# Convolutions of a graph network: the matmuls of a gathered group stand singly between the dense products

## The reference, cut to what matters

```
h   = x @ W                                   # 12500 nodes, 96 features
msg = dinv[row] * w * dinv[col] * h[row]      # 400,000 edges, sorted by destination
xc  = segment_sum(msg, col) + b
g   = sigmoid(x @ Wr + br)
x   = relu((1 - g) * x + g * xc)
```

## Time and profile before

| | |
|---|---|
| median of 3 runs | 11252.27 us (11244.29 to 11253.65) |
| the profiled execution | 11244.56 us, its span 11242.6 us |
| convolution stage, with both layers | about 5764 us to 11160 us of the span |
| TensorE busy over the span | 8235.0 us, 73% |
| GpSimd busy over the span | 6709.2 us, 60% |

### The profile page before, as it was taken

The page is one execution under the profiler, slowest core; times in us unless marked ns, Lnnn a source line. Parts: engine busy times, 40 slices in busy tenths (PEclk is TensorE's granted clock), DMA queues, the critical chain, the costliest instruction groups (busy, mean ns, idle before and its releaser), DMA issues.

```text
span 11242.6 us, 161615 instructions
## 1 busy us (share of the span) xinstructions
PE 8235.0 (73%) x40104; PEld 5614.5 (50%) x40104; DVE 5197.6 (46%) x17514; ACT 2896.6 (26%) x6502; POOL 6709.2 (60%) x6696
## 2 busy tenths in 40 slices
PE   5567666666767676667748888888875888888886
PEld 4334444444444444444435556555553555555554
DVE  5566666666666676666612222222231222222223
ACT  4345555555555555555300000000000000000000
POOL 4666565565566565656456666666645666666663
PEclk7678888888888888888768888888876988888887
DMA  4346566565566665656346666666664666666666
GB/s 151 81 132 175 166 175 172 167 174 168 171 174 175 172 176 172 172 168 174 128 144 230 229 236 237 228 232 233 228 205 152 232 225 235 231 233 232 232 229 204
DMA packets 1329034, 2149.88 MB, mean 191 GB/s; under 512 B 306427, under 2 KB 1079948, under 8 KB 1328700
## 3 DMA queue, kind: packets, MB, share of 16 engines
q10 hardware_dynamic: 142400, 986.64, 24.3%
q1 hardware_dynamic: 925996, 684.95, 20.7%
q0 software_dynamic: 260560, 477.49, 15.9%
HBM read 1587.45 MB, written 560.99 MB: 191 GB/s over the span
## 4 chain that ended last, share of the span: by engine, by line
PE 56%; issue 15%; another core or an unknown queue 15%; ACT 7%; DVE 3%; DMA 2%; POOL 1%; DVEq 1%; ACTq 1%; SPq 0%; POOLq 0%
PE bd L1159 30%; PE bd L1055 11%; PE sg L1146 6%; ACT blocks L1286 3%; PE pb L1044 3%; PE sg L1074 2%; PE pa L1044 2%; ACT hid L1265 2%; ACT msg L1278 1%; ACT gate_t L1271 1%; PE bd L1108 1%; PE bd L1171 0%; PE bd L1167 0%; DMA out_nodes<-s_c 0%
## 5 line engine op out<-in xcount | busy, mean ns | idle before, releaser
L909 POOL DMA_INDIRECT hid<-src_table,src_ids x3127 | 3188.8, 1020 | 2068.0 <-ACT msg L1278 1080.4
L1159 PE MATMUL bd<-ring,table_sb 128*96 128x280 f32 x13720 | 3580.3, 420 | 254.6 <-issue 145.1
L1159 PEld LDWEIGHTS bd<-ring,table_sb 128*96 128x96 f32 x13720 | 2332.5, 172 | 1408.7 <-issue 545.7
L1055 PE MATMUL bd<-one_hot_dst,one_hot_src 128*128 128x343 bf16 x8400 | 1751.2, 353 | 1449.9 <-ACT blocks L1286 1135.8
L953 POOL DMA_INDIRECT hid<-conv_table,hid x1724 | 1660.3, 963 | 1058.5 <-issue 512.4
L1055 PEld LDWEIGHTS bd<-one_hot_dst,one_hot_src 128*128 128x128 bf16 x8400 | 841.3, 108 | 2251.8 <-issue 1787.4
L1286 ACT ACTIVATE blocks<-bd 128x686 f32<-128x686 f32 x1400 | 1116.8, 798 | 2255.3 <-remote 1489.7
L953 POOL DMA_INDIRECT feat_in<-conv_table,hid x1152 | 1121.3, 973 | 618.3 <-issue 334.0
L1871 DVE TENSOR_TENSOR acc<-acc,sg 96x64 f32 x434 | 94.6, 218 | 2527.3 <-remote 1188.3
L1391 ACT ACTIVATE side_out<-bd,side_flag 96x280 f32<-96x280 f32 x70 | 34.3, 490 | 4022.5 <-issue 2294.1
L1885 DVE TENSOR_TENSOR acc<-acc,side_out 96x7 f32 x2800 | 469.6, 168 | 1256.2 <-issue 933.5
(11 more groups left out here) (226 smaller groups left out, 6957.8 us busy)
## 6 DMA issues: line engine op xcount, KB each, us to landing
ring<-adjacency ACTq DMA_DIRECT2D x980, 980.0 KB
adjacency<-blocks SPq DMA_DIRECT2D x700, 686.0 KB
attr<-in_attr SPq DMA_DIRECT2D x392, 128.0 KB
hid<-src_table,src_ids POOLq DMA_INDIRECT x3127
hid<-conv_table,hid POOLq DMA_INDIRECT x1724
feat_in<-conv_table,hid POOLq DMA_INDIRECT x1152
conv_table<-table_sb SPq DMA_DIRECT2D x28, 336.0 KB, 4.7
feat_half<-feat_keep SPq DMA_DIRECT2D x56, 168.0 KB
```

The source lines that it names most:

```text
L909: pool.indirect_dma_start(out=hid[s][:, t, :], out_offset=None, in_=src_rows, in_offset=bass.IndirectOffsetOnAxis(ap=src_ids[s // 2][:, j: ...
L1055: op = nc.tensor.matmul(bd[:, 512 * h:512 * h + HALF_Z], y[:, 1 + k, :], z[:, Z_PAD * h:Z_PAD * h + HALF_Z], start=(k == 0), stop=(k == 2))
L1159: op = nc.tensor.matmul(side_ps, table_sb[:, D * k:D * (k + 1)], ring[slot][:, :, QUAD_FANS * b:QUAD_FANS * (b + 1)], start=(k == 0), stop ...
```

## The change

Before, the eight matmuls of a group stand in a row behind a piece of seven dense products (behind pieces 1, 3, 6, 8, 10 and 13). In the changed kernel the loop runs over single products; behind every second one stands one matmul of a group. A group is thus spread over 16 products, six groups over 96, and products 96 and 97 have nothing behind them. The waits of a group stand before its first matmul, and `seg` is set by its eighth. The numbers of instructions, shapes, operands and buffers are the same, and so are the programs of the other engines.

```diff
-                    for t in range(GROUP):
-                        op = nc.tensor.matmul(sg[j][0:D, WINDOW * slot:WINDOW * (slot + 1)], conv_g[j][slot][:, t, :],
-                                              conv_s[j][slot][:, t, :], start=(t == 0), stop=(t == GROUP - 1))
-                    op.then_inc(s["seg"], 1)
+                    op = nc.tensor.matmul(sg[j][0:D, WINDOW * slot:WINDOW * (slot + 1)], conv_g[j][slot][:, t, :],
+                                          conv_s[j][slot][:, t, :], start=(t == 0), stop=(t == GROUP - 1))
+                    if t == GROUP - 1:
+                        op.then_inc(s["seg"], 1)
...
-                    for i in range(PIECES):
-                        piece(i, loaded)
-                        if i in SEGMENT_AFTER:
-                            m = SEGMENT_AFTER.index(i)
-                            unit_segment(m, u, n0)
-                            if mix and m == 0:
-                                mix_gate(h0 + u)
-                            if mix and m == 2:
-                                mix_own(h0 + u)
+                    for k in range(BLOCKS):
+                        product(k, loaded)
+                        m, turn = divmod(k, GROUP_BLOCKS)
+                        if m < UNIT_GROUPS and turn % BLOCKS_PER_TILE == BLOCKS_PER_TILE - 1:
+                            unit_tile(m, turn // BLOCKS_PER_TILE, u, n0)
+                        if mix and k == GROUP_BLOCKS:
+                            mix_gate(h0 + u)
+                        if mix and k == 3 * GROUP_BLOCKS:
+                            mix_own(h0 + u)
```

More of the change, by code:

```diff
@@ L99 @@
 RING = 7
-SEGMENT_AFTER = (1, 3, 6, 8, 10, 13)
+BLOCKS_PER_TILE = 2
+GROUP_BLOCKS = GROUP * BLOCKS_PER_TILE
 ADD_PARTS = 4
@@ L1150, in unit_segment, with segment_tile @@
-                def unit_segment(i, u, n0):
+                def segment_tile(t, k, j, m, slot, n0, s=cv[l]):
+                    if t == 0:
+                        if slot == 0 and not (isinstance(k, int) and k < 2):
+                            pe.wait_ge(s["acc"], n0 + group_of(k - 1, ACC_CREDIT))
+                        pe.wait_ge(s_rows[j][slot], rows_gathered(m, j, slot))
+                        pe.wait_ge(s["weighted"], n0 + group_of(k, slot + 1))
+                    op = nc.tensor.matmul(sg[j][0:D, WINDOW * slot:WINDOW * (slot + 1)], conv_g[j][slot][:, t, :],
+                                          conv_s[j][slot][:, t, :], start=(t == 0), stop=(t == GROUP - 1))
+                    if t == GROUP - 1:
+                        op.then_inc(s["seg"], 1)
@@ L1151, in unit_segment, with unit_tile, product @@
+                def unit_tile(i, t, u, n0):
                     k, slot = LEAD_STEPS + i // STEP_GROUPS, i % STEP_GROUPS
-                    segment(u * 2 + k, k % 2, u + k // 2, slot, n0)
-                def piece(i, loaded, s=cv[l]):
+                    segment_tile(t, u * 2 + k, k % 2, u + k // 2, slot, n0)
+                def product(k, loaded, s=cv[l]):
+                    i, b = divmod(k, PIECE_BLOCKS)
                     slot = i % RING
[L1156 to L1162, removed]
+                    if b == 0:
+                        pe.wait_ge(s_ring[slot], loaded * 32 + (16 * (i // RING) + 16))
+                    op = nc.tensor.matmul(side_ps, table_sb[:, D * k:D * (k + 1)],
+                                          ring[slot][:, :, QUAD_FANS * b:QUAD_FANS * (b + 1)],
+                                          start=(k == 0), stop=(k == BLOCKS - 1))
+                    if b == PIECE_BLOCKS - 1:
+                        op.then_inc(s["eaten"], 1)
@@ L1192, in _ @@
                         for slot in slots_of(k):
-                            segment(k, k % 2, k // 2, slot, n0)
+                            for t in range(GROUP):
+                                segment_tile(t, k, k % 2, k // 2, slot, n0)
                     with pe.Fori(0, HALVES) as u:
```

## The result

The changed kernel took 11339.97 us in the median of 4 runs (11337.22 to 11346.77), the kernel before 11248.63 in the median of 4 runs (11244.29 to 11253.65). It is slower: the medians differ by 91 us, or 0.81%. The ratio on record, another estimate from the same runs, is 1.0068 with an interval of 1.0045 to 1.0091, that is 76 us (51 to 102). The profiled execution took 11337.22 us, its span is 11335.3, so the difference of the spans is 92.7 us.

The account below looks back on a forecast made before the run. No engine was full; PE stopped whenever POOL gathered unbroken, costing some 18 us a unit. Tiles (-1.3) and bare copy (+1.33) cancel, earlier waits 0, rhythm +60: 11244.6 + 60 = 11305, about 11308 as median; range 11060 to 11450 us.

Parts of the forecast that it names:

- The verdict, slower: Whole kernel: time rises by more than 0.2% (22 us); chance 0.52, against 0.28 for faster.
- the rhythm of `seg`: Convolution units: evenly spaced `seg` settings lengthen POOL and PE's cycles of joined groups; +60 us taken.
- PE's own work: PE's undisturbed work per unit: tile gain and bare copy cancel, 54.5 us before and after.
- The unit's length: Convolution unit, measured from one ACT copy to the next: about 74.7 us after the change.
- The tile term: Gathered matmuls: standing alone, each takes about 0.14 us against 0.166 in a row; -1.3 us a unit.
- The term of the unit's end: Unit's last product: no row covers ACT's copy any more, 1.48 us idle in place of 0.15; +1.33.
- the cycle: POOL joins two groups, PE stops, POOL runs out of work, repeat: three groups take 38.5 us, up from 37.2.
- The rule of onset: While POOL gathers unbroken, PE lives on about 67 held records, then stops; all 79 runs of 16 had one.
- (1): Stops belong to rows of short matmuls, so spreading them gains: 10600 us at half, 10350 at best; 12%.
- (3): POOL's idle time absorbs what PE still has to do in a cycle: 11245 to 11265 us; 20%.
- (5): Three groups join often, PE crawls 20 us and five groups take 66 us: 11400 to 11500 us; 15%.
- (2): Lucky rhythm: mostly four-group cycles with one stop, part of -380 us, giving 11100 us; 16%.

Follow-up runs that it names:

- bare_copy: Kernel before with its sixth row behind the thirteenth piece instead of the last, leaving ACT's copy uncovered; 11361.97 us against 11271.59, ratio 1.0085.
- last_row_b: Changed kernel with a unit's sixth group left as a row of eight behind the last product, on a chip with stops; 1.0047 of the kernel before.
- old_rhythm_b: Changed kernel with single matmuls spread so each group ends behind its old product (14, 28, 49, 63, 77, 98), on a chip with stops; 1.006 of the kernel before.
- even_rows_b: Changed kernel with each group's eight matmuls again in a row, behind products 16, 32, ... 96, on a chip with stops; 1.004 of the kernel before.
- half_before: Kernel before with only four of a group's eight tiles gathered, each used twice; 9923.47 us, 0.8814 of the kernel before.
- ctrl_after: Changed kernel run again without edit, beside the kernel before on one chip with stops; 11334.85 us against 11260.99, ratio 1.0054.
- half_after: Changed kernel with only four of a group's eight tiles gathered, each used twice; 10005.85 us, 0.8887 of the kernel before.

## Why the prediction was right, and where it was not

The verdict, slower, was the one to which I gave the most, 11339.97 lies in the range, and it is 32 us over the forecast of 11308. The steps behind it did less well than the number, and that the number came so near is luck: its +60 is the rhythm of `seg`, which no run shows, and PE's own work, which was measured at +1.36 us a unit, stood in it as 0.

**The unit's length.** Forecast about 74.7 us, measured 74.8 and 75.0. But the forecast came from 0 for PE's work and +0.9 for the rhythm.

**The tile term was wrong.** "48 x 0.14 = 6.7 against 8.0 us, -1.3": it measured 0. The 0.14 is right, but I stopped the account at the start of the product behind the tile, and that product gives the gain back: 0.265 in place of 0.236. With it both sides are 48 x 0.170 = 8.2 us, for the row too has such a product behind it. The record ahead of a short one, and the one behind it, both belong to its price. The Trainium skill (TensorE: Matmul & The Clock Gate, Step-by-step) says that weights load under the matmul that runs; the trace agrees where that matmul is long. That the load behind a short one is what costs is my reading of the 0.085 and the 0.265, not something that a run took apart.

**The term of the unit's end was right.** "+1.33" measured 1.36. "The two terms cancel" is the sentence that failed: nothing cancels it, and where nothing stops PE and PE sets the pace, in the pair with half the gathers, it is the whole difference, 91 us. On the whole kernel the medians of bare_copy and of the result are apart by about as much (90 and 91 us), but with intervals of 60 to 131 and 51 to 102 us, and with 62 and 57 us of it between the copies. So the likeness of the three numbers is no proof.

**Whether PE's work counts while there are stops.** The prediction let PE's 54.5 us enter only through the cycle. bare_copy speaks against that: with no single tile it is as slow as the changed kernel. But that 1.36 us at a unit's end is felt in full between stops is not shown. In the result's trace the time lost in stops and at ends of units is the same as before (1013 and 1005 us), and the 57 us stand mostly in products at the lower clock. Which way the change leads there is open.

**The rhythm term, +60, isn't shown.** Its sign can't be read from the change itself, since bare_copy gives the whole loss with distances that are the old ones in another order. last_row_b, with the copy covered and five groups at the new distances, is slower by 0.5%, which speaks for some such cost. But the parts don't add. If single tiles, the bare copy and even distances each had a price of their own, last_row_b, old_rhythm_b and even_rows_b would make the whole change (.0047 + .0060 + .0040)/2 = .0074 and the bare copy .0027, where it measured .0085; and with .0085 for the copy, even distances would be worth -.0045 and single tiles -.0025, and last_row_b, which has both, would be faster. It is slower. (The half-widths of these ratios are .0016 to .0031, and the .0085 comes from another chip.) How the new distances and the joined runs of POOL work on each other is left open; the profiled executions differ too much among themselves for it (5356 and 5375 us for the same kernel).

**The stops.** The rule of onset was right for runs of 16 wherever there were stops, on three chips and in each kernel with all its gathers: they all had a stop, in the medians 12.2 to 13.8 us in, and PE went on 2.4 to 3.0 us behind them. For runs of 8 it is less clean: by one and the same count 13 of 197 have a stop in the kernel before, but 41 of 222 in even_rows_b. "Fewer of them but some of 20 us or more" was wrong: more and shorter, and their sum changed by 3% only. That it is a rule of "this kernel" was wrong as well: on one chip of four the same program ran without them. The Trainium skill (Runtime: NRT & Kernel Launch, Instruction fetch mechanics) calls fetching hidden; that agrees with the chip at 9195 us, and on the others nothing shows that the stops are fetches: in the kernel before, the profile has no load of instructions in the running loop of layer one. That PE lives on instructions that it holds is an argument from the 67 records alone. What is shown is that on the chips with stops they go when half of the gathers are left out, and come when POOL's runs last over 12 us.

**The rivals.** (1) is refuted by half_before. (3), "POOL fixes all", came true where I had not looked, on the chip without stops. (5) did not occur. (2) did not show.

**Not the change.** 35 of the 93 us between the two profiled spans arose before the changed stage. So the price of the change is not known closely; the measures of it go from 57 to 91 us: the copies give 57 us in the first profile and 76 in that of ctrl_after, the ratios 76 and 61 us, the medians 91 and 74.

## What to carry to other kernels

Look at what stands behind the last long matmul before a wait that comes back from another engine. A row of short matmuls there fills the round trip (here 1.71 us from last product to next), which then costs nothing more; spread out, the matmuls cost the same and the trip lies bare, 1.36 us each time. That is so where PE sets the pace, as in half_before and half_after; where POOL set it, at 9195 us, the bare trip cost nothing. And don't take numbers of like size for one cause: here 91, 90 and 91 us came from traces that lose the time in different places. When short matmuls are put between long ones, count the distance to the record behind them too. And before a rule is built on a stall with no cause in the profile, run the kernel before on another chip: here it took 18 to 20% less on one of four.

## What was not expected of the hardware

- The same program, with equal instruction counts and gathers 1.25 us apart, took 9195 us on one chip and 11261 to 11531 on three others. In the profile from the one, no stop came with POOL's runs, though 1725 gathers stood without a gap.
- While POOL gathers for over 12 to 14 us without a break, PE (and DVE) get one instruction about every 0.7 or 1.4 us, until 2.3 to 3.0 us behind the last gather. Runs of 8 gathers (9.8 us) mostly have none (13 of 197 in the kernel before, 41 of 222 in even_rows_b); of the 392 runs of 4 in half_before none has one.
- Of the records of short fp32 matmuls (64 columns), the first behind a long one (280 columns) has the next 0.056 us behind it, every other 0.085. The second long record behind a short one starts 0.265 us behind the first, in place of 0.236. A tile then costs 0.170 us, alone or in a row of eight.
